# Adding the second layer's value bias behind the output projection, and evicting V on ScalarE in both layers

## What is computed

```python
x = x + xattn(ln(x), ctx, ctx, L0)         # no biases
x = x + attn(ln(x)); x = x + ffn(ln(x))    # small layers of layer 0
# second layer
q = heads(ln(x) @ Wq.T + bq)
k = heads(ctx @ Wk.T + bk)
v = heads(ctx @ Wv.T + bv)
out = softmax(q @ k.T / sqrt(16)) @ v      # 16 heads of 16
x = x + (out @ Wo.T + bo)
x = x + ssm(ln(x)); x = x + moe(ln(x))     # scan with gelu; mixture of experts
```

## Time and profile before

| | |
|---|---|
| median of 3 runs | 1118.84 us (1117.42 to 1119.2) |
| the profiled execution, its own time | 1118.7 us |
| its span, first to last instruction | 1116.8 us |
| TensorE busy (matmul) | 1013.0 us, 91% |
| VectorE busy | 642.1 us, 57% |
| ScalarE busy | 562.8 us, 50% |
| GpSimd busy | 149.5 us, 13% |
| mean granted clock of TensorE | 0.954 |

### The profile page before, as it was taken

How to read it: one execution, slowest core, us unless ns; L and a number is a source line. 1 busy time by engine, 2 the same in 40 slices (tenths; PEclk the granted TensorE clock), 3 DMA queues, 4 the chain that set the end, 5 groups by cost and what they waited for, 6 DMA issues and landing times.

```text
span 1116.8 us, 31381 instructions
## 1 busy us (share of the span) xinstructions
PE 1013.0 (91%) x13428; PEld 660.1 (59%) x13428; DVE 642.1 (57%) x1062; ACT 562.8 (50%) x1012; POOL 149.5 (13%) x181
## 2 busy tenths in 40 slices
PE   4589889999999999999999999999638999999998
PEld 2256656666766666676666666666425444445887
DVE  4555646557475556657667666664457444436342
ACT  5177667676676576455566566555337322222110
POOL 4021111111111111111121121110000000000000
PEclk9699989999999999999999999998559999999999
DMA  6496374553644342354334444322201223222310
GB/s 217 114 304 186 97 215 101 152 155 89 177 98 141 97 112 63 106 114 123 82 97 112 94 114 112 83 63 115 76 1 38 76 78 112 82 107 79 112 39 20
DMA packets 72101, 121.54 MB, mean 109 GB/s; under 512 B 35046, under 2 KB 48518, under 8 KB 68762
## 3 DMA queue, kind: packets, MB, share of 16 engines
q1 hardware_dynamic: 71196, 117.86, 37.0%
q0 software_dynamic: 624, 1.60, 0.4%
q10 hardware_dynamic: 144, 0.07, 0.0%
HBM read 63.88 MB, written 16.26 MB: 72 GB/s over the span
## 4 chain that ended last, share of the span: by engine, by line
PE 78%; DVE 14%; ACT 4%; issue 3%; DMA 1%; POOL 0%; SPq 0%; DVEq 0%; ACTq 0%; POOLq 0%
PE ps L589 75%; DVE mpart L1167 4%; PE ps L831 1%; DVE rinv L1184 1%; DVE cl L1142 1%; PE ps L715 1%; ACT p L950 1%; ACT kh L928 1%; DMA sel<-in_sel 1%; ACT ch L911 1%; DVE oT L1187 1%; DVE st L1111 1%; ACT wh L961 0%; DVE wl L1198 0%; DVE qh L1311 0%
## 5 line engine op out<-in xcount | busy, mean ns | idle before, releaser
L1167 DVE TENSOR_REDUCE mpart<-ps 128x2 f32<-128x800 f32 (+1 forms) x256 | 252.5, 990 | 154.2 <-PE ps L589 153.1
L950 ACT ACTIVATE p<-ps 128x512 f32<-128x512 f32 (+1 forms) x416 | 225.3, 595 | 118.1 <-PE ps L589 116.1
L542 POOL TENSOR_TENSOR kl<-k,kh 128x400 f16<-128x400 f32 (+1 forms) x128 | 118.3, 924 | 519.4 <-ACT kh L928 519.2
L589 PE MATMUL ps<-p,v 128*17 128x64 f32 x6656 | 138.1, 226 | 0.6 <-DVE osum L1194 0.6
L589 PE MATMUL ps<-qcur,ks 97*128 97x128 f16 (+1 forms) x1664 | 133.8, 223 | 3.7 <-ACT p L950 2.6
L1198 DVE SCALAR_TENSOR_TENSOR wl<-w,wh 128x2048 f16<-128x2048 f32 x24 | 55.0, 2292 | 126.4 <-ACT wh L961 126.4
L589 PEld LDWEIGHTS ps<-p,v 128*17 128x17 f32 x6656 | 101.7, 100 | 40.1 <-issue 31.1
L589 PEld LDWEIGHTS ps<-qcur,ks 97*128 97x128 f16 (+1 forms) x1664 | 103.8, 101 | 30.5 <-issue 8.0
L589 PE MATMUL ps<-kh,qbcur 32*128 32x400 f16 (+1 forms) x512 | 89.8, 349 | 33.5 <-DVE mpart L1167 25.3
L589 PE MATMUL ps<-wvh,ch 128*128 128x256 f16 (+1 forms) x416 | 115.0, 276 | 4.6 <-ACT kh L928 3.6
L589 PE MATMUL ps<-wvl,ch 128*128 128x256 f16 (+1 forms) x416 | 114.1, 274 | 0.0
(11 more groups left out here) (205 smaller groups left out, 1427.0 us busy)
## 6 DMA issues: line engine op xcount, KB each, us to landing
ks<-kh SPq DMA_DIRECT2D x256, 100.1 KB
w<-in_wgu SPq DMA_DIRECT2D x16, 1024.0 KB, 4.8
ks<-kl SPq DMA_DIRECT2D x128, 100.1 KB
w<-in_wd SPq DMA_DIRECT2D x8, 1024.0 KB, 4.8
c32a<-in_ctxT SPq DMA_DIRECT2D x16, 400.5 KB, 4.6
cparts<-ch SPq DMA_DIRECT2D x8, 800.5 KB, 5.9
cparts<-cl SPq DMA_DIRECT2D x8, 800.5 KB, 7.4
c32a<-in_ctxT SPq DMA_DIRECT2D x12, 400.0 KB, 3.3
```

Of the source, the lines that this page charges most:

```text
L542: nc.gpsimd.tensor_tensor(kl[:, mt, k0:k0 + w], k32[:, ku % 2, 0:w], kh[:, mt, k0:k0 + w], ALU.subtract).then_inc(sem("klo_done"), 1)
L589: return nc.tensor.matmul(o, lhsT, rhs, start=start, stop=stop, skip_group_check=shared)
L950: nc.scalar.activation(p32[0:n, step % PRING, BANK * hb:BANK * hb + BANK], ps[0:n, hb, :], ACT.Exp, scale=DH ** -0.5).then_inc(sem("exp_do ...
L1167: nc.vector.reduce_max(mpart[:, j0:j0 + 2, quarter], o.rearrange("p (b c) -> p b c", b=2)[:, :, 0:w], AX.X).then_inc(sem("max_done"), 1)
```

## The change

`bv` is no longer added in the eviction of V. ScalarE evicts V in both layers. The value bias comes as a column tile `bv`, laid out like `oT`; an event `v_spread` behind step 3 of round 10 spreads it over 128 columns (VectorE), and an event `v_bias` behind step 5 multiplies it with `wo` (four f32 matmuls into `mid`), and VectorE adds the result to row 2 of `rows`, ahead of the first `out` of layer 1. `rows` is loaded with three rows in place of four, and `bv` is one more load in GpSimd's queue, ahead of `sel`.

```diff
+BIAS_AT = {(B + 2, 3): "v_spread", (B + 2, 5): "v_bias"}
...
+    if (g, k) in BIAS_AT:
+        found.append((BIAS_AT[g, k], 1, 0))
...
+            "v_bias": ("bias_added", 1)}.get(name)
...
-        rows = sb(ctx, "rows", [P, 4, D])
+        rows = sb(ctx, "rows", [P, 3, D])
+        bv = sb(ctx, "bv", [P, GROUPS])
...
+            with ExitStack() as s2:
+                bvs = sb(s2, "bvs", [P, GROUPS, P])
...
-                        load(rows[:, 0:2, :], d["rows"][:, 4:6, :], "gamma_in")
+                        load(rows[:, 0:2, :], d["rows"][:, 3:5, :], "gamma_in")
...
-            load(rows[:, :, :], d["rows"][:, 0:4, :], "const_in")
+            load(rows[:, :, :], d["rows"][:, 0:3, :], "const_in")
+            load(bv[:, :], d["bv"], "rw_in")
...
+                elif name == "v_bias":
+                    pe.wait_ge(sem("wo1_in"), 16)
+                    pe.wait_ge(sem("bv_spread"), 1)
+                    for e in range(GROUPS):
+                        last = mm(mid[:, 0:D], bvs[:, e, :], wo[:, e, :], e == 0, e == GROUPS - 1)
+                    last.then_inc(sem("bias_mm"), 1)
...
-                    pe.wait_ge(sem("rw_in"), 32)
+                    pe.wait_ge(sem("rw_in"), 48)
...
-                elif letter == "V" and layer == 0:
+                elif letter == "V":
                     kts = V_TILES[i]
...
-                if letter == "V" and layer == 1:
-                    kts = V_TILES[i]
-                    n = TILE_ROWS[kts[0]]
-                    dve.wait_ge(sem("v_mm"), V_UNITS * r + i + 1)
-                    need(dve, "pv_mm", KT * (r - 1) + kts[-1] + 1)
-                    nc.vector.scalar_tensor_tensor(
-                        v[0:n, kts[0]:kts[-1] + 1, :, 0:DH],
-                        o[0:n, 0:D * len(kts)].rearrange("p (k h d) -> p k h d", h=H, d=DH), 1 / W_SCALE,
-                        rows[0:n, 3, :].rearrange("p (h d) -> p h d", h=H).unsqueeze(1)
-                        .broadcast_to([n, len(kts), H, DH]), ALU.mult, ALU.add).then_inc(sem("v_done"), 1)
-                elif letter == "O":
+                if letter == "O":
                     divide(r, 0)
...
+                elif name == "v_spread":
+                    dve.wait_ge(sem("rw_in"), 48)
+                    nc.vector.tensor_copy(bvs[:, :, :], bv[:, :].unsqueeze(2).broadcast_to([P, GROUPS, P]))\
+                      .then_inc(sem("bv_spread"), 1)
+                elif name == "v_bias":
+                    dve.wait_ge(sem("bias_mm"), 1)
+                    nc.vector.tensor_tensor(rows[:, 2, :], rows[:, 2, :], mid[:, 0:D], ALU.add)\
+                      .then_inc(sem("bias_added"), 1)
+                    dve.wait_ge(sem("bias_added"), 1)
...
+    bv = np.zeros((4, 2 * DH, GROUPS), np.float32)
+    bv[:, 0:DH] = a["L1_xattn_bv"].reshape(GROUPS, 4, DH).transpose(1, 2, 0)
+    d["bv"] = bv.reshape(P, GROUPS)
```

More of the change, by code:

```diff
@@ L161, in event_read_by @@
             "f_gate": ("f_m", t + 1), "q_make": ("q32_done", TT * layer + t + 1), "s_u": ("scan", 7 * t + 1),
-            "s_y": ("gelu", t + 1), "r_logits": ("lgm_in", t + 1), "power": ("am_pow", t + 1)}.get(name)
+            "s_y": ("gelu", t + 1), "r_logits": ("lgm_in", t + 1), "power": ("am_pow", t + 1),
+            "v_bias": ("bias_added", 1)}.get(name)
 def users_before():
@@ L1472, in lay_out @@
     d["bias"] = np.stack([a["L1_xattn_bq"].reshape(2, P).T, a["L1_xattn_bk"].reshape(2, P).T], 1)
-    rows = np.stack([a["L0_attn_bo"], a["L0_ffn_bg"], a["L1_xattn_bo"], a["L1_xattn_bv"], a["L1_attn_gamma"],
-                     a["L1_attn_beta"]])
-    d["rows"] = np.broadcast_to(rows, (P, 6, D))
+    rows = np.stack([a["L0_attn_bo"], a["L0_ffn_bg"], a["L1_xattn_bo"], a["L1_attn_gamma"], a["L1_attn_beta"]])
+    bv = np.zeros((4, 2 * DH, GROUPS), np.float32)
+    bv[:, 0:DH] = a["L1_xattn_bv"].reshape(GROUPS, 4, DH).transpose(1, 2, 0)
+    d["bv"] = bv.reshape(P, GROUPS)
+    d["rows"] = np.broadcast_to(rows, (P, 5, D))
     d["sel"] = (np.arange(P)[:, None] == np.arange(P) // 32 * 32 + DH).astype(np.float32)
```

## The result

The changed kernel took 1120.5 us (median of 22 runs), the kernel before 1118.55 (22 runs, on the same chip). The ratio is 1.0016, with an interval of 1.0008 to 1.0023: 1.8 us slower. Forecast was 1118.8, no change against before; the time is inside the range, but that it would be slower was not foreseen. One run with a mean clock of 0.556 is left out.

What follows compares the result with a forecast made beforehand. TensorE, busy 91% of the span, was taken to bound the kernel, so only evictions on its waits counted. Gains and costs summed to -0.02 us against a median of 1118.84: forecast 1118.8, range 1116.4 to 1121.0.

Steps and rivals of the forecast that it cites:

- The clock: Granted clock fell after the stall at 464.19, worth 1.7 us; a fall may be lost or won, most of the spread.
- Rival (a): The clock fall at 464 in round 8 does not come: -1.7 us, 1117.1; chance 0.22.
- rival (c): Clock falls in round 11 or 13, where gelu lengthens a stall: 1120.5 if short, 1123.8 if long; chance 0.13.
- 8, start: At the start, the extra bv load delays sel and the first low part of the context: +0.40 us, bounds 0 and +1.1.
- 3, round 8: Round 8, step 6: without V6 the product starts ahead of GpSimd's kl and P waits less: -0.82 us.
- 1, round 9: Round 9, step 2: V leaves VectorE's chain and TensorE's wait for the sums ends: -0.17 us.
- 2 and 5, round 10 with the row: Round 10: a shorter wait for a maximum in step 1, -0.33, and the bias row's matmuls, +0.42 us.
- 6, spread: Round 10, after step 3's maximum: the 128x512 spread on VectorE, priced at 0.69 us, fits into idle time: 0.
- 7, gelu, rounds 11 and 13: V5 on ScalarE delays gelu's table load and gelu, ahead of TensorE's wait for the K eviction: +0.41 each, +0.82 us.
- 4 and 7, round 15: Round 15: V6 off the chain to the transposes, -0.34 us; gelu's delay of some 0.7 swallowed by TensorE's 2.15 wait.
- Step 5: Round 10: four bias-row matmuls, 1.61 us of issue, partly fill the stall ahead of P: +0.42 us.
- step 2: Round 10, step 1: TensorE's wait of 0.38 for a maximum shrinks by 0.33: -0.33 us.

Runs made afterwards that it cites:

- the control: The changed kernel run once more with no edit: 1120.71 us, ratio 1.0025 to the kernel before.
- the two delays: The kernel before with 6 or 12 filler matmuls on TensorE's path in round 10, step 9, where it has no stall: 1123.22 and 1121.65 us.
- the row alone: The changed kernel with all V of the second layer evicted by VectorE, scaled only, the bias row kept: 1118.52 us, ratio 1.0023 to the kernel before.
- before with round 8 filled: The kernel before with 6 filler matmuls in TensorE's stall of round 8, step 6, only: 1118.19 us, ratio 1.0009.

## Why the prediction failed, step by step

The failing step is the one headed **The clock**. The steps that were added up came out right in sum (+0.10 in place of -0.02, below); what made the changed kernel's first trace slower is 1.5 us ahead of round 8 and 4.0 behind round 15, in stages that the steps do not touch, at 1.2 GHz. It said "a fall may be lost or won; that is most of the spread", took the falls in rounds 8 to 15 for the only ones in play, and centred the forecast on the one profile of before. Three things in it were wrong. The largest stretch at half clock, from 796 on, was taken as given, though its end decides how much of the busy part of the mixture of experts runs at 1.2 GHz (0 or 7 us by the windows, up to 4.6 us of time by the table). Falls were taken as independent, while one filled stall only moved the fall to a later one. And faster and slower were given about the same chance (0.12 and 0.11), while the kernel before is well placed: all eight variants without fillers behind the rounds have ratios above 1 (1.0007 to 1.0044; for the two with one stall filled the interval holds 1), among them the one without the row, whose own steps make it 1.2 us quicker in round 10, and a delay made it slower by more than its length. Rival (a), the fall at 464 gone, and rival (c), a fall in round 11, both came, in both traces of the changed kernel (608 and 610). They were kept apart, with 0.22 and 0.13, yet without fillers a later fall came wherever the one at 464 was gone. That the median is just the 1120.5 of rival (c) is luck: (c) was worked out with the fall at 464 kept, and the control's trace, with (a) and (c) together, took 1118.73.

The steps before it, each with what the control showed against before (differences between the queries of neighbouring rounds; a fall's 1.47 taken off in rounds 8 and 11):

| step | forecast | measured |
|---|---|---|
| 8, start | +0.40 | -0.23 |
| 3, round 8 | -0.82 | -1.23 |
| 1, round 9 | -0.17 | -0.03 |
| 2 and 5, round 10 with the row | +0.09 | +0.30 |
| 6, spread | 0 | 0 |
| 7, gelu, rounds 11 and 13 | +0.82 | +0.88 |
| 4 and 7, round 15 | -0.34 | +0.41 |
| sum | -0.02 | +0.10 |

- **Step 3** was right in mechanism: the order of product and `kl` turned and the product took 0.29. It was larger: the wait for the maximum shrank by 0.91, and the 0.23 for which ScalarE's exponentials held TensorE in step 0 is gone; 0.09 is not placed.
- **Step 5**: the row begins where forecast, once the 0.33 of step 2 is counted, and it takes 2.37 from its first matmul to P's in place of 2.24. Without it, round 10 is 1.54 shorter.
- **Step 6** took 0.42, not up to 0.69, and is hidden; VectorE idles 1.74 behind it.
- **Step 7** was right in size and wrong in place: the wait is for `mid`, which gelu reads, not for the K eviction.
- **Steps 4 and 7 in round 15** were wrong: "TensorE's wait of 2.15 swallows that". It does not. The control shows a new wait of 0.63 for gelu, and the transposes come at 782.61, where before had 782.63, though the query of round 15 was 0.47 earlier:

```profile
772.06 0.70 PE L597 MATMUL ps<-osum,sel 128*128 128x256 f32 x2 [0.63 <-ACT g_a L1037]
...
782.61 0.66 PE L723 MATMUL ps<-ident,xm 128*128 128x128 f32 x2 [2.11 <-DVE xm L1132]
```

- **Step 8** had the wrong sign, below its lower bound of 0: the smaller `rows` was said to give nothing if earlier, yet 0.21 was left to gain beside a norm that was 0.52 later.

What stays open: which of the small shifts (0.23 earlier at the start, 1.23 in round 8) puts most runs of the changed kernel where they lose. A shift alone is enough to do it, as the two delays show; that it is this shift was only argued. Where the time of the runs without a trace went was not seen either. And why the runs of one program fall into groups, as in the row alone and in before with round 8 filled (eight runs to 1119.3, three from 1122.6), no run here tells.

## What to carry to other kernels

Compare two traces stage by stage, at landmarks that both have, before you explain a difference in time: here the loss between the two traces lay where the instructions were the same. In a kernel with stretches at half clock, a change of less than a microsecond can move the end by more than four (here, always the slower way); so test a small change with the clock held up (matmuls that compute nothing in the stalls), or against the same kernel delayed by as much. And such fillers were worth more than the change that was studied: 0.45% on the changed kernel behind the rounds alone, ahead of a stage that TensorE bounds, and 0.6 to 0.9% with those in the rounds.

## What was not expected of the hardware

- The same stage of the same instructions took 75.25 to 79.89 us; the granted clock is the difference that the windows show. In every trace without fillers there TensorE runs at 1.2 GHz for most of its first 40 us; what differs is when the clock rises for good.
- 0.64 us more on TensorE's path made the kernel 4.7 us slower, 1.28 us more 3.1.
- A stall of 1.79 us is followed by half clock in some cases and not in others: not at 562 in before, but in round 10 of the same kernel 1.8 us earlier.
- A copy of 128x512 f32 with a broadcast input took 0.42 us on VectorE, less than the eviction of V from PSUM at 0.69.
